# Pads of a routed feed-forward layer: plain transfers from ScalarE's queue in place of GpSimd scatters

## The reference, cut to what matters

```python
x = x + 0.5 * ffn(layernorm(x), ...)      # layer "m = 0"
x = x + attention(layernorm(x), ...)
x = x + 0.5 * ffn(layernorm(x), ...)      # layer "m = 1", same weights

def ffn(x):
    t = rmsnorm(x) * norm_w
    logits = t @ gate_w.T + gate_b        # 16 experts
    vals, idx = top_k(logits, 4)          # each token goes to 4 experts
    G = softmax(vals) put at idx          # 16 gates a token, 12 of them 0
    h = t @ w1[e].T + b1[e]               # per expert e
    act = a * sigmoid(1.702 * a) * (b + 1)    # a, b: even, odd columns of h, clipped
    y = act @ w2[e].T + b2[e]
    return x + sum over e of G[:, e] * y[e]
```

## Time and profile before

| | us |
|---|---|
| median of 3 runs | 1123.13 (1119.69 to 1123.15) |
| the profiled execution, its own time | 1121.11 |
| its span in the trace | 1119.4 |
| busy in the span: TensorE | 737.8 (66%) |
| VectorE | 622.3 (56%) |
| ScalarE | 425.2 (38%) |
| GpSimd | 370.7 (33%) |

### The profile page before, as it was taken

One profiled execution on the slowest core, in us unless ns is written; L12 is line 12 of the kernel. 1 busy time (PEld: TensorE's weight loads), 2 busy tenths in 40 slices (PEclk: granted clock), 3 DMA queues, 4 the chain that ended last, 5 costly groups with the idle time before them and its releaser, 6 DMA issues. The chain is left out here.

```text
span 1119.4 us, 22068 instructions
## 1 busy us (share of the span) xinstructions
PE 737.8 (66%) x5770; PEld 449.6 (40%) x5770; DVE 622.3 (56%) x1953; ACT 425.2 (38%) x945; POOL 370.7 (33%) x404
## 2 busy tenths in 40 slices
PE   2222169999999107658999998531205999999930
PEld 1112036666666003323343443421202666666620
DVE  6876036566665484446767672462502656665537
ACT  3433035555555012204545454110103555555510
POOL 4866723333333103440000000064772333333320
PEclk9999989999999657866999999755556999999975
DMA  9752323333332553420111100222232333333347
GB/s 321 253 211 94 118 75 91 87 96 89 91 88 83 188 169 95 131 76 16 45 31 35 33 27 3 76 87 72 98 113 72 92 93 96 94 93 92 83 146 230
DMA packets 110387, 114.31 MB, mean 102 GB/s; under 512 B 38836, under 2 KB 96669, under 8 KB 110272
## 3 DMA queue, kind: packets, MB, share of 16 engines
q1 hardware_dynamic: 95008, 73.82, 23.1%
q0 software_dynamic: 15264, 39.10, 9.4%
HBM read 60.89 MB, written 55.56 MB: 104 GB/s over the span
## 5 line engine op out<-in xcount | busy, mean ns | idle before, releaser
L322 POOL DMA_INDIRECT y_rows<-y_m,goal_m x158 | 155.6, 985 | 302.2 <-ACT y_m L486 282.9
L394 PE MATMUL banks<-w1s,rT_m 128*128 x948 | 234.6, 384 | 0.0
L671 DVE TENSOR_SCALAR b_m<-banks 128x256 f32<-128x256 f32 x158 | 67.1, 425 | 218.2 <-ACT p_m L472 110.3
L312 POOL DMA_INDIRECT x_rows<-row_m,row_to_m x128 | 135.0, 1054 | 121.2 <-DVE row_to_m L631 83.7
L1197 DVE CUSTOM_DVE_ANT_0 junk<-banks,maskq 128x128 bf16<-128x128 f32 (+3 forms) x256 | 115.6, 488 | 44.9 <-PE banks L1046 41.8
L465 ACT ACTIVATE rT_m<-banks 128x512 f16<-128x512 f16 x158 | 93.5, 592 | 105.4 <-issue 78.3
L394 PEld LDWEIGHTS banks<-w1s,rT_m 128*128 128x128 f16 x948 | 93.9, 99 | 97.5 <-issue 5.0
L416 PE MATMUL banks<-w2s,hT_m 128*128 x948 | 129.2, 273 | 0.0
L1166 ACT ACTIVATE probs<-banks 128x1024 f32<-128x1024 f32 (+3 forms) x128 | 86.1, 703 | 88.7 <-PE banks L1082 88.5
L376 PE MATMUL banks<-ident,rows_m 128*128 128x128 f16 x632 | 62.7, 223 | 79.2 <-DMA goal_m<-x_rows 40.0
L472 ACT ACTIVATE p_m<-banks 128x256 f32<-128x256 f32 x158 | 60.7, 384 | 116.7 <-PE banks L394 111.2
(11 more groups left out here) (165 smaller groups left out, 1160.4 us busy)
## 6 DMA issues: line engine op xcount, KB each, us to landing
rows_m<-x_rows SPq DMA_DIRECT2D x158, 128.0 KB
arena_m<-y_rows SPq DMA_DIRECT2D x32, 512.0 KB, 5.4
arena_m<-in_w SPq DMA_DIRECT2D x16, 512.0 KB, 7.4
arena_m<-in_w SPq DMA_DIRECT2D x16, 256.0 KB, 8.4
qk_split<-w_raw SPq DMA_DIRECT2D x32, 128.0 KB
x_rows<-pad SPq DMA_DIRECT2D x2, 2040.0 KB, 9.9
q_stack<-qk_split SPq DMA_DIRECT2D x32, 96.0 KB
k_stack<-qk_split SPq DMA_DIRECT2D x32, 96.0 KB
```

Of the source, the lines that this page charges most:

```text
L312: pool.indirect_dma_start(x_rows[m], bass.IndirectOffsetOnAxis(ap=row_to[:, i, k:k + 1], axis=0), row[:, i % NR, :], None).then_inc(scatte ...
L322: pool.indirect_dma_start(y_rows[m], bass.IndirectOffsetOnAxis(ap=goal[:, c, :], axis=0), y[:, n % NY, :], None, bounds_check=K * T - 1, o ...
L394: mm = pe.matmul(o, rT[:, n % 2, 2 * r + k, :], w1s[:, bass.ds(e, 1), k, w, :], start=False, stop=(k == HC - 1 and w == 1))
L671: dve.tensor_scalar(b[:, n % 2, :], bank[2 + n % 2][:, INNER:], (LIMIT + 1.0) * S, (1.0 - LIMIT) * S, ALU.min, ALU.max).then_inc(ev("b"), 1)
```

## The change

1. The 16 pad scatters leave GpSimd. ScalarE issues them instead as plain transfers of 128 consecutive rows, behind its routing work and ahead of `rows_out(0)`: for each expert it reads the first row number into a register (`value_load` of `pad_at`) and issues one transfer on its own queue. Each expert has its own semaphore `padded[e]`, and each of the slots 0 to 15 waits for that of its own number.
2. The table for the gelu is loaded by an explicit instruction ahead of those transfers.
3. The ranks of group g no longer count earlier groups with products. A tile `base[:, g, :]` starts as `region` and VectorE adds each group's counts to it, which TensorE leaves in 16 columns of bank 5 for each group. `locate(g)` adds `base[:, g, :]` where it added `region`. The number of products at L353 goes from 24 a layer to none; VectorE gets one copy and four additions of 128x16, each behind a wait for `counts`. `slots()` takes the totals from `base[:, B, :]`.
4. SyncE reads the table entries of slots 0 to 3 before it waits for the scatters.

```diff
-                PADS = (1, 2, 4, 8, 16)
-                padded = [ev(f"padded{j}") for j in range(len(PADS))]
-                pad_group = lambda e: next(j for j, last in enumerate(PADS) if e < last)
+                padded = [ev(f"padded{e}") for e in range(E)]
...
-                        def load_rows(n):
-                            c = n % NX
+                        def place_of(n):
                             row0 = sp.value_load(slot_tab[0:1, 0, n:n + 1], ...)
                             cell = sp.value_load(slot_tab[0:1, 1, n:n + 1], ...)
+                            return row0, cell
+
+                        def load_rows(n, row0, cell):
+                            c = n % NX
...
-                            if n < E and n in (0,) + PADS:
-                                sp.wait_ge(padded[pad_group(n)], 16 * (PADS[pad_group(n)] - n))
+                            if n < E:
+                                sp.wait_ge(padded[n], 16)
...
                         sp.wait_ge(ev("slot_tab"), 1)
+                        places = [place_of(n) for n in range(4)]
                         sp.wait_ge(ev("idle_made"), 16)
...
-                            load_rows(n)
+                            load_rows(n, *(places[n] if n < 4 else place_of(n)))
...
-                        pool.wait_ge(ev("pad_at"), 1)
-                        for e in range(E):
-                            pool.indirect_dma_start(x_rows[m], bass.IndirectOffsetOnAxis(ap=pad_at[:, e:e + 1], axis=0),
-                                                    pad[:, :], None).then_inc(padded[pad_group(e)], 16)
...
-                            for i in range(g * TPB):
-                                pe.matmul(bank[4][...], ones16[:, :], mask16[:, i:i + 1, :].broadcast_to([P, TPB, E]), ...)
...
-                                mm = pe.matmul(bank[5][:, 0:E], ones16[:, :], mask16[:, i, :], start=(i == 0),
-                                               stop=(i == NT - 1), skip_group_check=True)
-                            if g == B - 1:
-                                mm.then_inc(ev("counts"), 1)
+                                mm = pe.matmul(bank[5][:, g * E:(g + 1) * E], ones16[:, :], mask16[:, i, :], start=(t == 0),
+                                               stop=(t == TPB - 1), skip_group_check=True)
+                            mm.then_inc(ev("counts"), 1)
...
+                        act.preload_act_table_set("gelu_apprx_sigmoid_and_others")
+                        act.wait_ge(ev("pad_at"), 1)
+                        for e in range(E):
+                            first = act.value_load(pad_at[0:1, e:e + 1], min_val=0, max_val=(E - 1) * REGION + T)
+                            act.dma_start(x_rows[m][bass.ds(first, P), :], pad[:, :]).then_inc(padded[e], 16)
                         rows_out(0)
...
-                                              region[:, :].unsqueeze(1).broadcast_to([P, TPB, E]), ALU.add)\
+                                              base[:, g, :].unsqueeze(1).broadcast_to([P, TPB, E]), ALU.add)\
...
+                            dve.wait_ge(ev("counts"), g + 1)
+                            step(dve.tensor_tensor(base[:, g + 1, :], base[:, g, :], bank[5][:, g * E:(g + 1) * E], ALU.add))
...
-                            dve.wait_ge(ev("counts"), 1)
-                            step(dve.tensor_scalar(count[:, :], bank[5][:, 0:E], P - 1.0, None, ALU.add))
-                            dve.scalar_tensor_tensor(pad_at[:, :], bank[5][:, 0:E], place[:, 0:1], region[:, :],
-                                                     ALU.add, ALU.add).then_inc(ev("pad_at"), 1)
+                            step(dve.scalar_tensor_tensor(count[:, :], base[:, B, :], P - 1.0, region[:, :],
+                                                          ALU.add, ALU.subtract))
+                            dve.tensor_scalar(pad_at[:, :], base[:, B, :], place[:, 0:1], None, ALU.add)\
+                               .then_inc(ev("pad_at"), 1)
...
+                        step(dve.tensor_copy(base[:, 0, :], region[:, :]))
```

More of the change, by code:

```diff
@@ L166, in moe @@
                 pos = tmp("pos", [P, TPB, E])
+                base = tmp("base", [P, B + 1, E])
                 row_to = tmp("row_to", [P, NT, K], u32)
@@ L351, in rank @@
                                       skip_group_check=True)
-                            for i in range(g * TPB):
-                                pe.matmul(bank[4][:, 0:TPB * E].rearrange("p (t e) -> p t e", e=E), ones16[:, :],
-                                          mask16[:, i:i + 1, :].broadcast_to([P, TPB, E]), start=False, stop=False,
-                                          skip_group_check=True)
                             for t in range(TPB - 1):
```

## The result

The changed kernel takes 1096.34 us in the median of 4 runs (1095.43 to 1100.27), the kernel before 1123.14 us in 4 runs. The ratio is 0.9766, 95% interval 0.9732 to 0.9799: 26.8 us faster, where 37.3 were forecast.

What follows compares the result with a forecast made beforehand. Slots run at TensorE's pace, their start set by SyncE's slow spell. Earlier starts of 21.2 and 18.7 us give 39.9, or 34.6 with the tail; the middle, 37.3, from 1121.1 gives 1083.8 us, range 1076 to 1093.

Steps and rivals of the forecast that it cites:

- ScalarE partly slow: Pads on ScalarE: partly slowed by spells, or a new spell arises; 1093 to 1112 us, chance 0.22.
- What bounds: Second layer's slots: they run at TensorE's pace; SyncE's slow reads set their start, 24.3 us for two `load_rows`.
- What is removed: GpSimd's routing: 16 scatters fewer a layer, so its burst ends 20.4 us sooner, at 123.9 and 826.1.
- The start of the slots: `turn_rows(1)` at 831.9 instead of 853.12, saving 21.2 us; first layer's `up(2)` 18.7 us sooner; together 39.9.
- the tail: SyncE slow up to 5.4 us after GpSimd's last scatter: two slots some 2.6 us later in each layer.
- What ScalarE gets: Pads ahead of `rows_out(0)`: 1.08 us each, 17.3 for 16, covered by 2.0 us and 11.9 us of slack.
- The rival of the slow ScalarE: Pads at 6.1 us during GpSimd's bursts: 12.9 us saved, 1108; partly slow or new spell shared chance 0.22.
- The rival in which ScalarE's pads prolong the spell: ScalarE slow throughout, 97.6 us of pads a layer: 1228 us; chance of slower 0.08.
- The small parts: Ranks, VectorE additions, early table load: taken as 0; ranks and additions bounded −1.7 to +1.2 us a layer.
- The Trainium skill's rule on issuing engines: Pads moved between queues: if the rule's "small" held, nothing gained, 1121 us; chance 0.03.

## Why the prediction was right, and where its size was off

The time lies in the range given, but in the case given 0.22, ScalarE partly slow, and 3 us outside the forecast's own 1076 to 1093.

- **What bounds.** Right. Slots at TensorE's pace before and after; the pads alone carry the gain.
- **What is removed.** Right. The last token scatter ended at 121.6 (forecast 123.9) in the first layer; in the second, counted from the layer's start, 110.4 us (811.95 − 701.54), before 111.2 (826.1 − 714.93).
- **The start of the slots, up to `turn_rows(1)`.** Right within 2 us. (The 2.6 us a layer for the tail stand without their working; at the prediction's own rate in the spell, 1.08 / 6.1, its 3.9 us of tail would cost some 3.2.) Forecast with the tail of the spell 132.2, measured 130.42. In the second layer forecast 834.5, or 821.1 with the 13.4 us of the first taken off; measured 822.85.
- **What ScalarE gets.** Here the sum failed: "I take 1.08 because it is the common value of 158 slots". That value holds (1.04 measured), but nearly all of those slots run while GpSimd is not in a long run, and the pads are issued while it is. The pads took 23.85 and 38.72 us, so `rows_out(0)` ran some 5 us after its rows were there, in both layers. The sum put 6.3 us between `turn_rows(1)` and `up(2)`; they were 11.2 (141.58 − 130.42) and 11.5 (834.30 − 822.85). These 10.1 us are most of the 11.6 that the profiled span is short of the forecast (37.3 − 25.7); what the other 1.5 are stays open.
- **The rival of the slow ScalarE** was the right mechanism at too low a price a pad and too long a time. It took 6.1 us a pad, measured 8.4, because within its 24.3 us some instructions followed each other without the pause, the last ones above all; in exchange the measured first-layer spell was short, and TensorE waited 4.85 and 5.14 us for the pads, where the rival had them 14.4 and 12.6 us late. Its evidence was in the earlier trace rows: SyncE and VectorE were slowed, no row said that ScalarE is spared. The trace of before even shows ScalarE hit, in the third ranking stage (L is a line of the kernel before):

```profile
756.64 0.67 PE L332 MATMUL banks<-ident,u_m 128*128 128x128 f32 x2
...
776.67 0.38 ACT L500 ACTIVATE uT_m<-banks 128x256 f32<-128x256 f32 x1 [13.22 <-remote]
```

TensorE had turned the stage's last tile by 757.3, and ScalarE copied it at 776.67 after 13.22 idle us. VectorE's 14.78 us before 773.87 were no wait for a product either: that of its tile was done at 756.8. The 18 unharmed VectorE operations end 21 us into GpSimd's run of 785.17 to 846.54; they say nothing of the rest of the run.
- **Not its own pads.** The rival in which ScalarE's pads prolong the spell fell: the spell ended 4.5 us after GpSimd's last scatter with eleven pads still to go, and the breaks on GpSimd alone removed it.
- **The small parts**, taken as 0: beside the pads 0.5 us slower by the medians, 3.6 by the ratios, the intervals overlapping; 4 us faster without the move; 5 faster with the breaks, again with overlapping intervals. The 5.16 us before the ranks, which the prediction called a wait for them, were a stall. The early table load moved out of the first gelu's way and bought nothing that shows, as the rows of the second layer had it. In the Trainium skill, "ScalarE: Activation LUTs", section "What ACT_TABLE_LOAD costs", 2.66 us in all are counted for a switch of tables, the load and a drain. Here the load stands at 99.90 with 1.28 us, in ScalarE's idle time. A drain behind the load doesn't show: in the earlier trace rows the gelu starts 1.09 us after the load's end, as soon as `up` is done.
- **The Trainium skill's rule on issuing engines**, "DMA: Bandwidth & Descriptors", section "Issuing engines are not separate DMA queues", by which spreading only saves the time to issue, usually small: the gain here was 26.8 us by the whole change, and 22.9 where breaks keep the spell from the token scatters. It is not simply the 20.4 us of issue a layer: from 820 to 875 us in the kernel before SyncE's list of waits has 0.3 us, for a result's buffer, and none for a pad. What the scatters' issue cost was the slow stretch that it laid over the first slots.

The better version that came out is the changed kernel with one break of GpSimd behind each tile's scatters: 1075.32 and 1076.5 us, ratios 0.96 and 0.9591, against 0.9766 of the change.

## What to carry to other kernels

When a queue crawls, look at instructions that touch nothing: an 18 ns assertion that takes 700 ns shows that the queue itself is slow, which a list of waits doesn't. Look at the pauses between instructions too; here they were as long again. A price taken from calm rows doesn't hold for work that is issued in such a stretch. Long rows of indirect transfers on GpSimd are worth breaking up: a few tenths of a microsecond of extra spacing every fourth scatter made the whole kernel some 20 us faster. An issue moved off a busy engine still delays everything behind it on the new one, so put ahead only what the first consumers need.

## What the runs showed of the hardware

- With scatters (128 rows of 1088 bytes each) issued by GpSimd at a pitch of 1.28 us in long unbroken runs, the instruction streams of ScalarE and SyncE fell to about 0.7 us an instruction, whatever the instruction, with as much again between two: 1.4 us each. In the second layer of the changed kernel this began at 791, 20 us into the run of 771.18 to 811.95; in the first at 114.3, 37 us into the run of 77.66 to 121.62. So no fixed onset shows, and engines are not hit together: VectorE stood from 97.45 to 101.84 in that first layer, while ScalarE worked through 97 to 101 without a pause.
- It ended at 816.5, 4.5 us behind the run, and at 123.9, 2.3 us behind it.
- A mean pitch of 1.47 us kept it from ScalarE's and SyncE's streams in the changed kernel, and from SyncE's in the kernel before, where ScalarE still stalled once for 3.53 us; 1.39 us ((760.45 − 754.89) / 4) removed the hole of 11.9 us ahead of the third ranking stage's scatters and kept the first layer's pads free of it, but over the second layer's pads the spell stayed in one profile (40 us for the 16) and nearly vanished in the other (18 us); a memset that left the pitch at 1.28 us did nothing.
- Why other engines slow down, whether by their instruction fetch or something else that the scatters' descriptors load, no run here shows. Nor was the pitch varied finely enough for a threshold.
- Outside the spell a register read and a transfer with its address from a register cost ScalarE 1.04 us, of which the transfer instruction is 0.34.
